# Attention block on one core: the places of the matmul operands in SBUF, by 256 bytes

## What is computed

```python
q = einsum('bchw,dc->bdhw', x, theta_w) + theta_b      # 256 x 1024 per image
xpool = maxpool2(x)                                    # 1024 x 256
k = einsum('bchw,dc->bdhw', xpool, phi_w) + phi_b      # 256 x 256
v = einsum('bchw,dc->bdhw', xpool, g_w) + g_b          # 256 x 256
p = softmax(einsum('bdn,bdm->bnm', q, k) * 256 ** -0.5)
vp = einsum('bdm,bnm->bdn', v, p)
out = einsum('bdhw,cd->bchw', vp, z_w) + z_b + x
```

## Time and profile before

| | |
|---|---|
| median of 3 runs | 2065.04 us |
| the profiled execution, whole | 2064.01 us |
| its span, first to last instruction | 2061.0 us |
| mean granted TensorE clock | 0.996 |
| TensorE matmul busy | 2035.9 us, 99% |
| VectorE, GpSimd, ScalarE busy | 76%, 67%, 63% |

### The profile page before, as it was taken

How to read it: one execution, slowest core, us unless ns; L and a number is a source line. 1 busy time by engine, 2 the same in 40 slices (tenths; PEclk the granted TensorE clock), 3 DMA queues, 4 the chain that set the end, 5 groups by cost and what they waited for, 6 DMA issues and landing times.

```text
span 2061.0 us, 49045 instructions
## 1 busy us (share of the span) xinstructions
PE 2035.9 (99%) x17816; PEld 2032.3 (99%) x17816; DVE 1558.4 (76%) x2620; ACT 1299.3 (63%) x2228; POOL 1374.8 (67%) x833
## 2 busy tenths in 40 slices
PE   8899999999999999999999999999999999999997
PEld 8899999999999999999999999999999999999997
DVE  8787777787777877777877778777778777787765
ACT  6666566666666665666766666656666656666653
POOL 4676666776676766667766667766677666677643
PEclk9999999999999999999999999999999999999999
DMA  6656556656566565566565665555665655655635
GB/s 225 202 174 206 177 200 224 205 185 214 170 213 234 175 208 183 187 224 218 179 214 173 204 233 180 207 193 178 219 231 170 212 176 209 224 194 193 206 102 183
DMA packets 212907, 407.27 MB, mean 198 GB/s; under 512 B 12688, under 2 KB 15760, under 8 KB 212880
## 3 DMA queue, kind: packets, MB, share of 16 engines
q1 hardware_dynamic: 212736, 406.90, 58.2%
q10 hardware_dynamic: 144, 0.01, 0.0%
HBM read 272.64 MB, written 134.22 MB: 197 GB/s over the span
## 4 chain that ended last, share of the span: by engine, by line
PE 95%; DVE 3%; POOL 1%; DMA 1%; issue 1%; ACT 0%; SPq 0%; DVEq 0%; POOLq 0%
PE bank L835 94%; DVE pt_raw L652 1%; DMA x<-x 1%; POOL x_split_lo L534 0%; DVE x_top L670 0%; DVE x_bot L670 0%; DVE g_lo L616 0%; POOL att_lo L552 0%; POOL att_f L547 0%; DVE pooled L624 0%; PE bank L842 0%; ACT probs L441 0%; DVE att_f L683 0%; DVE att_f L681 0%; POOL pt_lo L544 0%
## 5 line engine op out<-in xcount | busy, mean ns | idle before, releaser
L534 POOL TENSOR_TENSOR x_split_lo<-x,x_split_hi 128x1024 fp32r<-128x1024 f32 x255 | 614.8, 2417 | 248.5 <-ACT x_split_hi L338 242.5
L835 PE MATMUL bank<-x_split_hi,theta_hi 128*128 128x256 f32 x2048 | 566.6, 277 | 3.5 <-POOL x_split_lo L534 1.9
L835 PE MATMUL bank<-x_split_lo,theta_hi 128*128 128x256 f32 x2048 | 566.5, 277 | 0.0
L835 PE MATMUL bank<-x_split_hi,theta_lo 128*128 128x256 f32 x2048 | 566.4, 277 | 0.0
L835 PE MATMUL bank<-att_hi,z_hi 128*128 128x256 f32 x1792 | 496.6, 277 | 8.3 <-DVE x_bot L670 4.9
L835 PE MATMUL bank<-att_hi,z_lo 128*128 128x256 f32 x1792 | 495.7, 277 | 0.0
L835 PE MATMUL bank<-att_lo,z_hi 128*128 128x256 f32 x1792 | 495.6, 277 | 0.0
L652 DVE STREAM_TRANSPOSE pt_raw<-probs 32x256 f32<-32x256 f32 x1024 | 446.0, 436 | 20.7 <-ACT probs L441 4.1
L670 DVE TENSOR_TENSOR x_top<-bank,x_top 128x512 f32<-128x512 f32 x512 | 334.6, 687 | 73.2 <-PE bank L835 68.9
L835 PEld LDWEIGHTS bank<-x_split_hi,theta_hi 128*128 128x128 f32 x2048 | 385.5, 188 | 3.9 <-issue 3.9
L552 POOL TENSOR_TENSOR att_lo<-att_f,att_hi 128x512 fp32r<-128x512 f32 (+1 forms) x192 | 282.8, 1479 | 159.6 <-ACT att_hi L377 159.6
(11 more groups left out here) (71 smaller groups left out, 4339.8 us busy)
## 6 DMA issues: line engine op xcount, KB each, us to landing
x<-x SPq DMA_DIRECT2D x256, 512.0 KB, 3.9
x_top<-x SPq DMA_DIRECT2D x128, 512.0 KB, 6.9
x_bot<-x SPq DMA_DIRECT2D x128, 512.0 KB, 5.2
out<-x_top SPq DMA_DIRECT2D x128, 512.0 KB, 3.6
out<-x_bot SPq DMA_DIRECT2D x128, 512.0 KB, 6.5
x_top<-theta_wt SPq DMA_DIRECT2D x4, 256.0 KB, 5.6
x_top<-g_wt SPq DMA_DIRECT2D x4, 256.0 KB, 5.3
x_bot<-z_wt SPq DMA_DIRECT2D x4, 256.0 KB, 5.9
```

What stands on the lines that cost most here:

```text
L534: nc.gpsimd.tensor_tensor(flat(lo), flat(x_chunk(s, c)), raw(flat(hi)), ALU.subtract).then_inc(x_ready, 1)
L835: last = nc.tensor.matmul(dst, stationary(a), moving(b), start=start and n == 0, stop=stop and n == len(PRODUCTS) - 1, skip_group_check=re ...
```

## The change

Nothing is computed or ordered in another way. The tiles are allocated in another order and with other pads. All matmul operands have sizes of a multiple of 256 bytes in each partition, so a tile's start within 256 bytes is set by the pads and by the group of small tiles ahead of it. Counted in lines of 64 bytes within 256 bytes (0 to 3), by the words of the change for after and by the same sizes for before:

| stage | stationary tile, line before and after | moving tile, line before and after |
|---|---|---|
| K | phi: 1, 3 | xp: 0, 2 |
| A | vt: 0, 3 | pt: 3, 2 |
| S | q: 0, 2 | k: 3, 1 |
| V | xp: 0, 2 | g: 3, 1 |
| Q | theta: 0, 0 | x_split: 3, 3 |
| O | z: 0, 0 | att: 3, 3 |

Within every stage a tile's high and low part stand at the same line, and every slice that a matmul takes begins at a multiple of 512 bytes in its tile. The tiles behind the operands (x, x_top, x_bot, pooled, probs, pt_raw, att_f, still) start at line 1 before and at line 0 after.

```diff
-        sb("pad_a", [P, 16], f32)
-        att = [sb(f"att_{s}", [P, 7, HB], f32r) for s in ("hi", "lo")]
-        k = [sb(f"k_{s}", [P, DT, M], f32r) for s in ("hi", "lo")]
-        gw = [sb(f"g_{s}", [P, KT, D], f32r) for s in ("hi", "lo")]
-        xs = [[sb(f"x_split_{s}{i}", [P, KC, H], f32r) for s in ("hi", "lo")] for i in range(XS)]
+        xp = [sb(f"xp_{s}", [P, KT, M], f32r) for s in ("hi", "lo")]
         pt = [sb(f"pt_{s}", [P, MT, H], f32r) for s in ("hi", "lo")]
+        q = [sb(f"q_{s}", [P, DT, H], f32r) for s in ("hi", "lo")]
         bias = sb("bias", [P, NB], f32)
...
         rowinv = sb("rowinv", [P, NT], f32)
 
-        sb("pad_b", [P, 32], f32)
+        k = [sb(f"k_{s}", [P, DT, M], f32r) for s in ("hi", "lo")]
+        gw = [sb(f"g_{s}", [P, KT, D], f32r) for s in ("hi", "lo")]
+        sb("pad_a", [P, 32], f32)
+        phi = [sb(f"phi_{s}", [P, KT, D], f32r) for s in ("hi", "lo")]
+        vt = [sb(f"vt_{s}", [P, MT, D], f32r) for s in ("hi", "lo")]
+        att = [sb(f"att_{s}", [P, 7, HB], f32r) for s in ("hi", "lo")]
+        xs = [[sb(f"x_split_{s}{i}", [P, KC, H], f32r) for s in ("hi", "lo")] for i in range(XS)]
+        sb("pad_b", [P, 16], f32)
         theta = [sb(f"theta_{s}", [P, KT, D], f32r) for s in ("hi", "lo")]
         zw = [sb(f"z_{s}", [P, 7, TB * P], f32r) for s in ("hi", "lo")]
-        vt = [sb(f"vt_{s}", [P, MT, D], f32r) for s in ("hi", "lo")]
-        q = [sb(f"q_{s}", [P, DT, H], f32r) for s in ("hi", "lo")]
-        xp = [sb(f"xp_{s}", [P, KT, M], f32r) for s in ("hi", "lo")]
-        sb("pad_c", [P, 16], f32)
-        phi = [sb(f"phi_{s}", [P, KT, D], f32r) for s in ("hi", "lo")]
```

## The result

The changed kernel takes 2095.71 us (2094.13 to 2096.94, 4 runs) against 2064.82 us before: a ratio of 1.0152, 95% interval 1.0136 to 1.0167. It is slower by 1.5%, where 0.36% faster was forecast and the range ended at 2088. Its profiled span is 2092.3 us.

A forecast was written before the change was run, and what follows sets the result against it. TensorE was taken to bound the kernel, its matmuls running without a wait for 94% of the span. Terms of -6.5, -0.6, -2.1 and +1.8 us sum to -7.4, from 2065.04 to 2057.6 us; range 2055 to 2088 us.

The forecast's parts named there:

- two rhythms: TensorE's steady matmul spacing, fast at 113.3 ns or slow at 117.7 ns, each holding until something knocks it over.
- d: Line of the stationary tile minus that of the moving tile being read, modulo 4; 1 was claimed to keep the rhythm.
- Term 1: K becomes fast, 48 matmuls from 117.7 to 113.3 ns: 0.21 us for each of 31 images, -6.5 us.
- term 2: The A behind K needs no recovery to the fast rhythm: 30 x 0.02 us, -0.6 us.
- d = 0 makes it fast: Rule read from the border K into A: d = 0 turns slow into fast, at a cost of 0.02 us.
- term 4: Six new borders with d = 0 or 3 an image cost 0 to 0.02 us each; middle taken, +1.8 us.
- term 3: The beginning's slow rhythm ends at 95.07 instead of 157.26 us, by d = 0 at A into S: -2.1 us.
- Both slow rivals: d = 3 turning fast into slow, 2107 us, and the four moved stages running slow, 2085 us; chance 0.20 each.
- 2107: Time in us if d = 3 at V into Q and S into Q makes Q and O slow; chance 0.20.
- The second rival: The four moved stages run slow, by their place or by d = 0 met in the fast rhythm: 2085 us, chance 0.20.
- all 16944 matmuls at 117.7 ns: Case within the moved-stages rival where Q and O are slow too: some 65 us more, 2130 us, chance 0.02.
- 113.4 to 113.5: Sign that the forecast is right: mean ns a matmul over some 16900 in one piece of the chain, instead of 114.0.

## Why the prediction was wrong

The reading of what bounds the kernel held: TensorE without a wait, two rhythms, each holding itself, knocked over at borders by d. The run with all places two lines on and the one with V freed from xp show it, and the latter gives terms 1 and 2: -0.23 us an image computed, -0.23 measured once no border knocks.

The step that failed is the reading of K into A, "d = 0 makes it fast". In the trace of before d = 0 was met without a wait only in the slow rhythm, 30 times, and I made a direction of it. It is a turn: fast becomes slow as well (A into S at 160.17 us, from 2.72 to 2.83 for 24 matmuls). So does d = 3 (S into Q at 194.65, 21.20 us for 180). The gap in the sum was in term 4: "from above 0.02 us each" bounded the cost of a knock by that of a recovery, and left out that a knock from fast leaves a stage slow. The right upper bound was that of the next border, 24 to 180 matmuls at 4.4 ns, 0.1 to 0.8 us.

Term 1 came true in the changed kernel (K 5.45 us instead of 5.65), and term 2 too, A behind K lasts 2.72 us. So did the size of term 3, by luck: the second image took 2.3 us more than a steady one before and takes 0.1 more now. But the way to it was another. A behind the gap drew the fast rhythm this time, and the d = 0 ahead of S made S slow and not fast. All three are lost in 228 more slow matmuls of an image. Term 4, forecast at +1.8 us, was about +39, since an image is 1.07 us longer where terms 1 and 2 took 0.23 off it, and 1.30 x 30 = 39.

Both slow rivals were half right. d = 3 does turn fast into slow (S into Q, 180 matmuls), but V into Q meets a slow rhythm and turns it fast, so 2107 was too much. And d = 0 met in the fast rhythm makes slow, so S, V and the second A are slow as in the 2085 of the other, 96 of its 144 matmuls; the 180 of Q and O lie on top. The second rival named this very turn, at a chance of 0.20, but let its slow rhythm end ahead of Q and O. The range missed the result because it was cut between two rivals that happened together. Two lesser figures were off in themselves: all 16944 matmuls at 117.7 ns are 62.5 us more than now and not 65, and the forecast's own sum comes to 113.6 ns a matmul, not 113.4 to 113.5. Nothing rests on either.

The Trainium skill, in "SBUF — State Buffer", section "Who interferes with whom", calls TensorE's read ports for the moving operand and for the weights independent and says that TensorE never waits on anyone. For the other engines the traces agree: in the loop of the kernel before no step from one matmul to the next is longer than 0.122 us, and an image repeats to 0.01 us, with VectorE busy 76% beside it. For the two operands against each other they don't: their places alone moved the image from 62.79 to 64.82 us. That the delay arises at the ports isn't shown by any run.

## What to carry to other kernels

What follows is shown for this kernel alone, fp32r matmuls of 256 columns behind a weight load each. There, give the stationary and the moving operand of every stage the same distance modulo 256 bytes (one line of 64 was good), and look at the borders too: the new stationary tile against the old moving one. Where one border has to break the pattern, break it back at the next one and with few matmuls between; count the knocks around the loop, since those of d = 0 and d = 3 turn the rhythm and don't set it. And a behaviour that a trace shows from one side only, however many times, has no bound on the other side.

## What was not expected of the hardware

- A product of three matmuls has three slow rhythms that differ in which matmul takes 284 cycles and not 282, and they answer differently to d = 3.
- With d = 0 inside a stage a matmul takes 120.0 ns (288 cycles), with d = 2 118.5 on the mean of K; with d = 3 113.3 where K was entered from the fast rhythm and 117.7 where it was entered from the slow one.
- An fp32r matmul of 128 columns takes 111.7 ns, one of 256 columns 113.3, a bf16 one of 192 columns 83, and one small matmul of 64 columns fp32r or 32 columns bf16 put between two fp32r ones costs 0.12 to 0.13 us.
- A slow rhythm lasts as long as nothing knocks: with K and V alone moved, 504 of the 552 matmuls of an image, image after image.
